# Mixer border: the next batch's tokens normalised on ScalarE, key highs spread ahead of the lows, four output buffers, and 71 expert tiles

## The reference, cut to what matters

```python
h = _layernorm(x) * (1 + ca) + sa                      # modulated tokens
xn = _layernorm(h, ln1_g, ln1_b)
q, k, v = split(xn @ W_qkv)                            # 16 heads of 16, window 64 and the one before
o = softmax(band(q @ k.T / 4)) @ v
g = sigmoid(xn @ W_g + b_g)
y_ssm = scan(A, xn @ B_w + xn @ W_u + b_u) @ C_w       # s = A * s + u, along the tokens
x1 = h + g * (o @ W_O + b_O) + (1 - g) * y_ssm
x2 = x1 + gelu(_layernorm(x1, ln2_g, ln2_b) @ mlp_W1 + mlp_b1) @ mlp_W2 + mlp_b2
x = x + ga * x2
h = _layernorm(x) * (1 + cb) + sb
weights, sel = top_k(h @ gate_w, 2)
x = x + gb * sum_k(softmax(weights)_k * expert_{sel_k}(h))   # expert: D -> 2F, swiglu, F -> D
```

## Time and profile before

| | us |
|---|---|
| median of 3 runs | 1871.93 (1871.29 to 1875.77) |
| the profiled execution, its own time | 1873.2 |
| its span, first to last instruction | 1871.4 |
| TensorE busy (share of the span) | 1672.6 (89%) |
| VectorE busy | 1402.7 (75%) |
| GpSimd busy | 1061.6 (57%) |
| ScalarE busy | 916.1 (49%) |
| mean granted clock of TensorE | 0.967 |

### The profile page before, as it was taken

One profiled execution on the slowest core, in us unless ns is written; L12 is line 12 of the kernel. 1 busy time (PEld: TensorE's weight loads), 2 busy tenths in 40 slices (PEclk: granted clock), 3 DMA queues, 4 the chain that ended last, 5 costly groups with the idle time before them and its releaser, 6 DMA issues. The chain is left out here.

```text
span 1871.4 us, 64384 instructions
## 1 busy us (share of the span) xinstructions
PE 1672.6 (89%) x22640; PEld 1289.7 (69%) x22641; DVE 1402.7 (75%) x3235; ACT 916.1 (49%) x1706; POOL 1061.6 (57%) x1304
## 2 busy tenths in 40 slices
PE   4899999999999999789999999916999999999996
PEld 2666666666666666556666666615888888888886
DVE  7788888888888888558889888863666666666665
ACT  3344444444444444455566555503555555555553
POOL 5333333333333333345888888863666666666664
PEclk8899999999999999999999999958999999999998
DMA  5333333333333332335455544415777777667674
GB/s 160 105 95 95 95 96 96 95 89 91 96 96 96 96 96 78 89 132 175 138 151 147 163 125 137 141 35 107 133 135 135 132 132 131 128 129 133 126 130 73
DMA packets 249210, 216.60 MB, mean 116 GB/s; under 512 B 116548, under 2 KB 225799, under 8 KB 248896
## 3 DMA queue, kind: packets, MB, share of 16 engines
q1 hardware_dynamic: 194816, 138.61, 28.9%
q0 software_dynamic: 36352, 56.78, 16.4%
q10 hardware_dynamic: 17856, 18.37, 2.9%
HBM read 109.14 MB, written 62.38 MB: 92 GB/s over the span
## 5 line engine op out<-in xcount | busy, mean ns | idle before, releaser
L1974 POOL DMA_INDIRECT out<-experts_y,experts_entry x144 | 235.9, 1638 | 153.8 <-DVE experts_y L1950 120.1
L860 ACT ACTIVATE mixer_prob<-mixer_sc 128x1024 f32<-128x1024 f32 x128 | 131.3, 1026 | 197.4 <-PE mixer_sc L705 197.4
L1893 ACT ACTIVATE experts_g<-experts_pg,x_b 128x256 f32<-128x256 f32 x288 | 120.9, 471 | 204.8 <-PE experts_pv L132 202.9
L1915 DVE TENSOR_SCALAR experts_v<-experts_v 128x512 f32<-128x512 f32 x144 | 64.8, 450 | 185.6 <-ACT experts_v L1893 185.6
L130 PE MATMUL experts_pg<-experts_xT,x_w 128*128 128x256 f16 x576 | 157.9, 274 | 38.7 <-DMA experts_xT<-experts_rows 33.1
L1964 POOL DMA_INDIRECT experts_rows<-scratch_xs,experts_entry x144 | 153.8, 1068 | 67.7 <-issue 49.6
L1607 POOL DMA_INDIRECT scratch_queue<-mlp_entry,mlp_slot x128 | 158.6, 1239 | 41.5 <-issue 36.7
L991 DVE TENSOR_REDUCE w_mx<-mixer_sc 128x8 bf16<-128x1024 f32 x128 | 155.8, 1218 | 21.6 <-PE mixer_sc L679 21.3
L130 PE MATMUL experts_py<-x_w,experts_hh 128*128 x576 | 157.0, 273 | 2.0 <-DVE experts_hl L1927 2.0
L131 PE MATMUL experts_pg<-experts_xT,x_w 128*128 128x256 f16 x576 | 157.6, 274 | 0.0
L132 PE MATMUL experts_pg<-experts_xT,x_w 128*128 128x256 f16 x576 | 157.6, 274 | 0.0
(11 more groups left out here) (368 smaller groups left out, 5373.2 us busy)
## 6 DMA issues: line engine op xcount, KB each, us to landing
...
```

The lines of the kernel that those rows point to most:

```text
L860: act.activation(prob[:, n % 2, :].rearrange("p (c j) -> p c j", c=2), sc[:, 2:4, :], ACT.Exp, scale=SCALE).then_inc(exped.sem, 1)
L1893: act.activation(dst[:, q, f * ROWS:(f + 1) * ROWS], bank[:, q, f * ROWS:(f + 1) * ROWS], fn, bias=x["b1"][:, bass.ds(e, 1), bias + 2 * q ...
L1915: dve.tensor_scalar(v[:, q, :], v[:, q, :], -8.0, 10.0, ALU.max, ALU.min).then_inc(v_cut.sem, 1)
L1974: pool.indirect_dma_start(out=out, out_offset=bass.IndirectOffsetOnAxis(ap=entry[:, s, t, 0:1].bitcast(I32), axis=0), in_=y[:, s % 2, t, : ...
```

## The change

1. The next batch's x is normalised by ScalarE (`normalize_x`: four `Identity` activations, scale `rs`, bias `off`), after it has copied out the values and ahead of step 0, instead of by VectorE. For the bias GpSimd makes `off` = -mean * root in two more small operations after the first root; `off` has two halves, and the counter of the roots is counted evenly (`ROOTS`).
2. The keys are spread in two parts of four DMAs: the high parts as soon as they are there, at the end of the previous body and ahead of the store of x1, the low parts at the start of the body. TensorE waits for the high queries, the keys' low parts (which free the bank) and the high spread before window 0's scores by query, for the low queries before the gates, and for the low spread before the first scores by key.
3. `on` has four buffers for two.
4. The experts run over 71 tiles; the last group of the loop has five.

```diff
--- before.py
+++ after.py
...
@@ -420,7 +421,7 @@
         ve = m.sb("ve", [P, 2 * TT])
         rs = m.sb("rs", [P, 2 * TT])
         nt = m.sb("nt", [P, 2 * TT])
-        off = m.sb("off", [P, TT])
+        off = m.sb("off", [P, 2 * TT])
         xTf = m.sb("xTf", [P, KD, L])
 
         Qh = m.sb("Qh", [P, 2, NW, 2, WIN], F16)
@@ -434,7 +435,7 @@
         stl = m.sb("stl", [P, L], F16)
         prob = m.sb("prob", [P, 2, PAIRS * P])
         rden = m.sb("rden", [P, 2, KD, WIN])
-        on = m.sb("on", [P, 2, KD, WIN])
+        on = m.sb("on", [P, 4, KD, WIN])
         oTh = m.sb("oTh", [P, 2, L], F16)
         oTl = m.sb("oTl", [P, 2, L], F16)
         mix = m.sb("mix", [P, TT, D])
...
@@ -474,6 +475,7 @@
         k_hi = m.counter("k_hi", 2)
         k_lo = m.counter("k_lo", 2)
         k_spread = m.counter("k_spread", 64)
+        k_low_spread = m.counter("k_low_spread", 64)
         v_mm = m.counter("v_mm", 2)
         v_sb = m.counter("v_sb", 2)
         v_moved = [m.counter(f"v_moved{u}", 32) for u in range(2)]
@@ -535,13 +537,21 @@
                 row = scratch["mod"][bass.ds(b, 1), 0:2 * D].rearrange("a (i d) -> a i d", i=2)
                 sp.dma_start(shsc[:], row.to_broadcast([P, 2, D])).then_inc(x_in.sem, 16)
 
+            def spread_keys(part, done):
+                for j in range(4):
+                    r = slice(32 * j, 32 * j + 32)
+                    sp.dma_start(Kz[r, j % 2, part, :, WIN:], Kt[r, part, :, :]).then_inc(done.sem, 16)
+
+            def spread_high_keys(b):
+                sp.wait_ge(k_hi.sem, k_hi.at(b, 2))
+                spread_keys(0, k_spread)
+
             def body(b, more):
                 if isinstance(b, int) and b == 0:
                     sp.wait_ge(start.made.sem, 3)
+                    spread_high_keys(0)
                 sp.wait_ge(k_lo.sem, k_lo.at(b, 2))
-                for j in range(4):
-                    r = slice(32 * j, 32 * j + 32)
-                    sp.dma_start(Kz[r, j % 2, :, :, WIN:], Kt[r, :, :, :]).then_inc(k_spread.sem, 16)
+                spread_keys(1, k_low_spread)
                 if isinstance(b, int) and b == 0:
                     start.store_bias_rows(sp)
                 sp.wait_ge(x1_sb.sem, x1_sb.at(b, 0))
@@ -574,6 +584,8 @@
                         store_n1(b - 1, 2 * n - 12)
                 if more:
                     load_modulation(b + 2)
+                if not (isinstance(b, int) and b == NB - 1):
+                    spread_high_keys(b + 1)
                 sp.wait_ge(x1_sb.sem, x1_sb.at(b, TT))
                 sp.dma_start(scratch["x1"][bass.ds(b, 1), :, :].rearrange("a (t p) d -> p (a t) d", p=P),
                              x1[:]).then_inc(x1_out.sem, 16)
@@ -666,7 +678,8 @@
 
                 var = 1 if n == 0 else 0
                 if n == 0:
-                    pe.wait_ge(q_lo.sem, q_lo.at(b, 4))
+                    pe.wait_ge(q_hi.sem, q_hi.at(b, 4))
+                    pe.wait_ge(k_lo.sem, k_lo.at(b, 2))
                 else:
                     pe.wait_ge(maxed.sem, maxed.at(b, n))
                 for h in range(2):
@@ -687,6 +700,8 @@
                 pe.wait_ge(maxT_sb.sem, maxT_sb.at(b, n + 1))
                 if n > 0:
                     pe.wait_ge(exped.sem, exped.at(b, n))
+                else:
+                    pe.wait_ge(k_low_spread.sem, k_low_spread.at(b, 64))
                 var = 1 if n == 0 else 0
                 for h in range(2):
                     r = half_rows(h)
@@ -769,6 +784,7 @@
                         scores_by_query(b, s)
                     if s == 0:
                         made_once(b, (start.low, 6), (start.bsplit, 16 * 9))
+                        pe.wait_ge(q_lo.sem, q_lo.at(b, 4))
                         gates(b, 0)
                     if s == 1:
                         pe.wait_ge(drive_sb.sem, drive_sb.at(b, 1))
@@ -817,12 +833,19 @@
 
             def normalize_x1(b, tiles):
 
-                done = (NB, NEWTON) if isinstance(b, int) and b == NB - 2 else (b + 2, 2 * NEWTON)
-                act.wait_ge(s_rstd.sem, s_rstd.at(done[0], done[1] + SHIFT))
+                done = (NB, ROOTS) if isinstance(b, int) and b == NB - 2 else (b + 2, 2 * ROOTS)
+                act.wait_ge(s_rstd.sem, s_rstd.at(*done))
                 act.wait_ge(x1_out.sem, x1_out.at(b + 1, 0))
                 for t in tiles:
-                    act.activation(x1[:, t, :], x1[:, t, :], ACT.Identity, bias=off[:, t:t + 1],
+                    act.activation(x1[:, t, :], x1[:, t, :], ACT.Identity, bias=off[:, TT + t:TT + t + 1],
                                    scale=rs[:, TT + t:TT + t + 1]).then_inc(n1_sb.sem, 1)
+
+            def normalize_x(b):
+                act.wait_ge(s_rstd.sem, s_rstd.at(b, ROOTS))
+                act.wait_ge(xT_mm.sem, xT_mm.at(b, 0))
+                for t in range(TT):
+                    act.activation(nrm[:, t, :], x[:, t, :], ACT.Identity, bias=off[:, t:t + 1],
+                                   scale=rs[:, t:t + 1]).then_inc(s_norm0.sem, 1)
 
             def high_keys(b):
                 for c in range(2):
@@ -853,6 +876,8 @@
                     act.copy(blocks[:, :, 0:4:3, :],
                              v_bank[u].rearrange("p (m a d) -> p m a d", m=2 * PAIRS, a=2)
                              ).then_inc(v_sb.sem, 1)
+                if not last:
+                    normalize_x(b + 1)
                 for s in steps:
                     if 0 <= s - 1 < NW:
                         n = s - 1
@@ -867,7 +892,7 @@
                     if 0 <= s - 3 < NW:
                         n = s - 3
                         act.wait_ge(o_norm.sem, o_norm.at(b, n + 1))
-                        act.copy(oTh[:, :, WIN * n:WIN * n + WIN], on[:, n % 2, :, :]).then_inc(oT_hi.sem, 1)
+                        act.copy(oTh[:, :, WIN * n:WIN * n + WIN], on[:, n % 4, :, :]).then_inc(oT_hi.sem, 1)
                     if s in (6, 7) and not (isinstance(b, int) and b == 0):
                         normalize_x1(b - 1, (2 * s - 12, 2 * s - 11))
                     if s == NW + 1 and not last:
...
@@ -930,9 +955,6 @@
                 moments(dve, b, x, range(TT))
             if part == 1:
                 aggregate(dve, b, 0)
-            if part == 2:
-                dve.wait_ge(xT_mm.sem, xT_mm.at(b, 0))
-                normalize(dve, b, x, 0, s_norm0)
             if part == 5:
                 dve.wait_ge(s_h.sem, s_h.at(b, 2))
                 moments(dve, b, h, (0, 1))
@@ -983,8 +1005,6 @@
                     for j in range(3, 6):
                         start.low_part(dve, j, start.low)
                     start.negate(dve)
-                if not last:
-                    layer_norms(dve, b + 1, 2)
                 for s in steps:
                     if s < NW:
                         dve.wait_ge(q_scores.sem, q_scores.at(b, 2 * s + 2))
@@ -996,9 +1016,9 @@
                         dve.wait_ge(pv_mm.sem, pv_mm.at(b, n + 1))
                         dve.reciprocal(rden[:, n % 2, :, :], pvT[n % 2][:, 1, :, :]).then_inc(recip.sem, 1)
                         dve.wait_ge(recip.sem, recip.at(b, n + 1))
-                        if n > 1:
-                            dve.wait_ge(oT_lo.sem, oT_lo.at(b, n - 1))
-                        dve.tensor_tensor(on[:, n % 2, :, :], pvT[n % 2][:, 0, :, :], rden[:, n % 2, :, :],
+                        if n > 3:
+                            dve.wait_ge(oT_lo.sem, oT_lo.at(b, n - 3))
+                        dve.tensor_tensor(on[:, n % 4, :, :], pvT[n % 2][:, 0, :, :], rden[:, n % 2, :, :],
                                           ALU.mult).then_inc(o_norm.sem, 1)
                     if not first:
                         if s == 1:
...
@@ -1086,13 +1106,13 @@
                 done = 0 if isinstance(b, int) and b == NB else half
                 pool.wait_ge(s_seed.sem, s_seed.at(b, SEED * (done + 1)))
                 cols = columns_of(b, half)
-                refine_inverse_root(pool, s_rstd, b, NEWTON * done, ve[:, cols], rs[:, cols], nt[:, cols], pool_passed)
-                if cols.stop > TT:
-                    n = NEWTON * (done + 1)
-                    pool.tensor_tensor(off[:], mv[:, TT:, 0], rs[:, TT:], ALU.mult).then_inc(s_rstd.sem, 1)
-                    wait_alone(pool, s_rstd.sem, s_rstd.at(b, n + 1), pool_passed)
-                    pool.tensor_scalar(off[:], off[:], -1.0, None, ALU.mult).then_inc(s_rstd.sem, 1)
-                elif half == 1:
+                refine_inverse_root(pool, s_rstd, b, ROOTS * done, ve[:, cols], rs[:, cols], nt[:, cols], pool_passed)
+                shifts = slice(0, TT) if half == 0 and cols.start == 0 else slice(TT, cols.stop)
+                if shifts.stop > shifts.start:
+                    pool.tensor_tensor(off[:, shifts], mv[:, shifts, 0], rs[:, shifts], ALU.mult).then_inc(s_rstd.sem, 1)
+                    wait_alone(pool, s_rstd.sem, s_rstd.at(b, ROOTS * done + NEWTON + 1), pool_passed)
```

(22 more changed lines are left out.)

11 lines of the change are left out of this document (6 added, 5 removed).

## The result

| | us |
|---|---|
| median of 8 runs, changed kernel | 1863.85 (1856.73 to 1868.43) |
| median of 8 runs of the kernel before, beside them | 1872.26 |
| ratio | 0.9945, 95% interval 0.9927 to 0.9962 |
| the profiled execution, its own time; its span | 1862.49; 1860.7 |
| TensorE, VectorE, ScalarE, GpSimd busy | 1670.6, 1369.1, 937.5, 1047.0 |

A forecast was written before the change was run, and what follows sets the result against it. TensorE was taken to bound the experts outright and the mixer but for 8% lost at batch borders. 14 borders by 1.65 (23.1), last batch 6.9 and tile 8.03 sum to 38.0 us: 1833.9 us, range 1826 to 1852.

The forecast's parts named there:

- The tile: Experts: 71 tiles for 72 take away one tile's 8.03 us, bounds 7.9 and 8.1.
- steps 1 to 5: Mixer border in batch 3, followed from GpSimd's root through normalisation, modulation and statistics to window 2: gain 1.5 us.
- The turns that the two engines take: Mixer border: VectorE's scan and GpSimd's modulation exclude each other; with the scan ahead, second modulation takes 2.35 us, not 3.15.
- step 5: Mixer after window 2: VectorE's waits of 0.39 and 0.16 go, gain grows from 0.95 to 1.5 us and stays.
- The spread, forecast at no cost: SP queue at mixer borders: high keys, x1 store, low keys, then store of h, landing at 195.4 in time; no cost.
- a margin of 0.4 us: Batch 3: store of h lands at 195.4, GpSimd's first modulation needs it at 195.8.
- about when TensorE first needs them: Batch 3: low keys land near 194, with 1.5 us of TensorE idle time in window 2 behind.
- The last batch and the buffers: Four output buffers: 6.9 us in the last batch, window 4's output coming earlier, and 0.15 at each other border.
- A: Mixer border: GpSimd's second modulation stays at 3.15 us, a border gains 0.85; 1845.0 us, chance 0.13.
- B: Window 2: TensorE's clock falls after the new stretch at eleven more borders, costing 8.8 us; 1842.7 us, chance 0.15.
- C: Mixer border gives nothing: ScalarE or store of h 1.5 us late; tile and last batch remain, 1857 us, chance 0.11.
- D: Mixer border: slow SP queue delays the store of h; slower than before from 2.7 us lateness, 1890 at 4.0; chance 0.05.

The follow-up runs named there:

- the run of the other order without the other parts: Kernel before with only the split key spread, queued high keys, store of h, low keys, x1 store: ratio 1.0011, 2.1 us slower.

## Why the prediction was wrong

- **The tile:** forecast 8.03, measured 7.9. Right.
- **Normalisation and what follows, steps 1 to 5:** the mechanism was right in each step: no idle time before the transposition in window 0, the scan at 1.22, the second modulation at 2.36, the new stretch in window 2. The turns that the two engines take were confirmed from both sides, since the long pair (1.99 and 3.15) is there again where the modulation starts within the scan, as in the run of the other order without the other parts, and the short one comes wherever the scan lies ahead. Such turns are what the Trainium skill describes in SBUF — State Buffer, "Who interferes with whom"; this trace agrees: 1.99 and 3.15 us side by side, 1.22 and 2.36 apart. The size at window 3 was right too, with the spread away: 22.46 less 20.93 is 1.53, forecast 1.5. It then did not stay, as step 5 said it would: 0.28 of it goes in windows 4 to 7, and 0.66 in the changed kernel. That is the first failed step. These windows were said to take TensorE's own time, 2.84 us each, and they do not. In the changed kernel the cause is shown, instruction blocks that come late, mostly beside the loads; with the old spread the loads were not taken away, and there it is carried over. (The working looked at one batch; the mean of windows 4 to 7 before, 11.71 for 11.36, already had 0.35 to show.)
- **The spread, forecast at no cost:** this is the step that failed most. It costs 12.4 us alone and 19.3 in the changed kernel (0.9842 against 0.9945). The queue was worked out nearly right (7.5 against 8.1 us for the issue of the store), but a margin of 0.4 us was taken as a price of nothing, and the gaps between the groups were put at too little. The lateness of the modulation is a mean of 0.41 us (11.52 against 11.11 after the start of the batch), and window 3 loses 0.69. Half of that is the clock: the four batches in which it falls come to window 3 after 22.45 us, the other ten after 21.29, for 20.93 without the spread. So 0.36 of the 0.69 is there without any fall, and 0.33 comes from the four falls. Also, "about when TensorE first needs them" hid a wait for the low keys in 9 batches.
- **The last batch and the buffers:** forecast 6.9 and 14 by 0.15, together 9; alone 3.7. The trace has 4.65 at the last output and 4.66 at the first product of the MLP: the step that took the distance of two outputs of before as the gain counted a slow stretch as removed which only moved. In the changed kernel that batch gains less still (52.3 us up to the first product of the MLP, 47.8 with the buffers alone, 52.8 before), because its low keys land late. TensorE's wait in window 0 and the clock:

```profile
760.87 0.39 PE L708 MATMUL mixer_sc<-w_twoI,w_maskq 64*128 64x512 bf16 x2 [2.12 <-DMA w_Kz<-mixer_Kt]
```
```profile
760.00:761.00 1.00, 0.13 (x2) 0.14 (x4) 1.00 (x3) 0.00 (x0) 0.00 (x0) 1.00 1.09 291
761.00:762.00 1.00, 1.00 (x28) 0.92 (x26) 1.00 (x4) 0.00 (x0) 0.00 (x0) 0.78 1.03 217
762.00:763.00 1.00, 1.00 (x15) 0.68 (x10) 0.03 (x1) 0.39 (x1) 0.00 (x0) 0.50 1.03 209
```

  The stall of about 3 us ahead of the output remained, 2.99, as forecast.
- **The rivals:** A did not happen. B happened in four batches; it was priced with a stretch as long as the old one, and came with a longer one (1.94 to 2.02 us in those four; the fall at 383.30 of the earlier trace rows, put at batch 6, is batch 7's by the count of this text). C, "the store of h is later than worked out", was the nearest, at 1857 and with a chance of 0.11; D had the mechanism, a queue too slow for its readers, but set its point of decision at 2.7 us of lateness. The truth lies between C and D. None of them had the instruction supply, which the forecast had only as "short gaps in TensorE's issue that could go as well", on the side of a gain. That C's 1857 lies nearest is luck in part: window 2 doesn't start as before, as C has it, but 0.7 us earlier (17.94 for 18.66), and the time is lost behind it and in the last batch.
- **The sum, from the traces:** without the spread the span would be 1841.7. The spread adds 15.1 in the 14 batches (9.7 up to window 3, 5.4 in windows 4 to 7), 0.2 ahead of them, and 3.7 behind them: 5.0 in the last batch, less 1.3 in MLP and experts, which the spread doesn't touch (the MLP alone takes 470.2 to 475.1 us in the traces of this text): 1860.7. The way from the forecast's 38.0 to the 29.7 without the spread: the 14 batches give 17.2 for 23.1, the stretch ahead of them is 0.9 longer, and what is behind them gives 13.4 for 14.9.

What stays open: of the spread's 12.4 us alone, the trace shows only 4.5, while in the changed kernel it shows 20.3 up to the first product of the MLP (801.56 for 781.26), near the 19.3 of the runs; why four whole transfers beat eight halves in good order by 9.7 us in the changed kernel and by 2.1 alone was followed into the longer windows 4 to 7 but not taken apart. And the three parts without the spread sum to 22.3 us when made alone, but give 29.6 together; with intervals of 2.4 to 3.7 us either way on each, this is at the edge of what the runs can tell. In the traces the mixer doesn't have this difference: its end, taken at the first product of the MLP, comes 17.4, 4.7 and 0.1 us earlier with the normalisation, the buffers and the tiles alone, together 22.2, and 21.8 earlier with all three.
